# Reordering VectorE and ScalarE work in an attention unit: times-v ahead of the split of q and k, the maximum behind the blocks of q

## What is computed

```python
# layer 0 (layers 1 and 3: no rope, an rmsnorm of q and k instead)
q = (query @ Wq).reshape(nb, q_len, H, D).transpose(0, 2, 1, 3)
k = (key @ Wk).reshape(nb, q_len, KVH, D).transpose(0, 2, 1, 3)
v = (value @ Wv).reshape(nb, q_len, KVH, D).transpose(0, 2, 1, 3)
q = q * cos + _rotate_half(q) * sin
k = k * cos + _rotate_half(k) * sin
scores = jnp.einsum('bhqd,bhkd->bhqk', q, k) / jnp.sqrt(jnp.float32(D))
scores = jnp.where(mask == 0, jnp.float32(-1000000000.0), scores)
attn = jax.nn.softmax(scores, axis=-1)
x = jnp.einsum('bhqk,bhkd->bhqd', attn, v)
return x.transpose(0, 2, 1, 3).reshape(nb, q_len, H * D) @ Wo
```

## Time and profile before

| | us |
|---|---|
| median of 3 runs | 2640.58 |
| lowest, highest | 2638.4, 2644.09 |
| the profiled execution | 2624.64 |
| its span, first to last instruction | 2622.8 |
| PE busy | 2339.1 (89%) |
| DVE busy | 1885.0 (72%) |
| POOL busy | 1551.6 (59%) |
| ACT busy | 1228.2 (47%) |

### The profile page before, as it was taken

The page is one execution under the profiler, slowest core; times in us unless marked ns, Lnnn a source line. Parts: engine busy times, 40 slices in busy tenths (PEclk is TensorE's granted clock), DMA queues, the critical chain, the costliest instruction groups (busy, mean ns, idle before and its releaser), DMA issues.

```text
span 2622.8 us, 40547 instructions
## 1 busy us (share of the span) xinstructions
PE 2339.1 (89%) x12225; PEld 1935.5 (74%) x12225; DVE 1885.0 (72%) x3505; ACT 1228.2 (47%) x3610; POOL 1551.6 (59%) x1624
## 2 busy tenths in 40 slices
PE   5899999989889999999787888799779999999977
PEld 4787777777677888888665777676567888887753
DVE  4677777777877788888775776564377888887762
ACT  2444444444334666666433545323235666665421
POOL 4577777765325677777444666432446777776443
PEclk8899999999999999999899999899989999999989
DMA  3256667665324555555420000149714555554354
GB/s 106 76 188 212 214 212 221 213 198 173 102 73 146 172 178 170 174 173 179 154 68 30 1 1 17 62 153 345 253 57 142 179 178 175 177 173 150 114 200 148
DMA packets 296365, 390.33 MB, mean 149 GB/s; under 512 B 20977, under 2 KB 195697, under 8 KB 293210
## 3 DMA queue, kind: packets, MB, share of 16 engines
q1 hardware_dynamic: 280416, 338.60, 39.7%
q0 software_dynamic: 10224, 42.03, 4.7%
q10 hardware_dynamic: 5514, 7.11, 0.8%
HBM read 269.92 MB, written 151.49 MB: 161 GB/s over the span
## 4 chain that ended last, share of the span: by engine, by line
DMA 16%; POOL 14%; DVE 13%; PE 11%; issue 10%; ACT 4%; SPq 0%; ACTq 0%; DVEq 0%; POOLq 0%
DMA q_in<-between_q 5%; PE B_qkv L841 5%; DMA between_q<-xn 4%; DMA slots_y<-S 3%; POOL qT_l L2252 3%; POOL W L2292 2%; POOL ring_l L2228 2%; DVE ss L1614 2%; DVE qk L1643 2%; DMA out_x<-rows_last 2%; DVE S L1700 1%; DVE S L1697 1%; DVE xn L1666 1%; POOL rn L2239 1%; PE B_out L841 1%
## 5 line engine op out<-in xcount | busy, mean ns | idle before, releaser
L1376 ACT ACTIVATE W<-S,nmx 128x128 f32<-128x128 f32 x768 | 298.5, 395 | 79.3 <-DVE nmx L1703 78.7
L2292 POOL TENSOR_TENSOR W<-W,rden 128x512 f32<-128x512 f32 x192 | 199.8, 1040 | 215.8 <-DVE rden L1708 215.7
L2298 POOL TENSOR_TENSOR pT_l<-W,pT_h 128x512 fp32r<-128x512 f32 x184 | 238.6, 1297 | 48.7 <-ACT pT_h L1197 48.4
L1718 DVE STREAM_TRANSPOSE S<-W 128x512 f32<-128x512 f32 x184 | 130.6, 710 | 189.0 <-POOL W L2292 189.0
L2252 POOL TENSOR_TENSOR qT_l<-q_in,qT_h 128x512 fp32r<-128x512 f32 x156 | 202.6, 1299 | 88.1 <-ACT qT_h L1197 86.7
L2228 POOL TENSOR_TENSOR ring_l<-raw,ring_h 128x512 fp32r<-128x512 f32 x166 | 216.0, 1303 | 61.2 <-ACT ring_h L1197 60.8
L841 PE MATMUL B_out<-ring_h,oT_h 128*128 128x512 f32 x516 | 211.9, 411 | 16.3 <-DVE oT_l L1522 9.5
L898 PE MATMUL B_s<-kT,qT_h 128*128 128x256 f32 x768 | 198.5, 336 | 30.8 <-DVE xnT_l L1522 13.4
L841 PE MATMUL B_out<-ring_h,oT_l 128*128 128x512 f32 x516 | 203.3, 394 | 0.0
L841 PE MATMUL B_out<-ring_l,oT_h 128*128 128x512 f32 x516 | 202.9, 393 | 0.0
L898 PEld LDWEIGHTS B_s<-kT,qT_h 128*128 128x128 f32 x768 | 147.6, 192 | 65.9 <-issue 42.4
(11 more groups left out here) (504 smaller groups left out, 7820.3 us busy)
## 6 DMA issues: line engine op xcount, KB each, us to landing
raw<-in_pieces SPq DMA_DIRECT2D x270, 256.0 KB, 3.0
between_q<-xn SPq DMA_DIRECT2D x156, 320.0 KB, 3.0
q_in<-between_q SPq DMA_DIRECT2D x156, 320.0 KB, 3.3
between_p<-S SPq DMA_DIRECT2D x184, 256.0 KB, 2.7
W<-between_p SPq DMA_DIRECT2D x184, 256.0 KB, 2.8
slots_x<-in_zero SPq DMA_DIRECT2D x32, 1030.0 KB, 7.3
raw<-in_experts SPq DMA_DIRECT2D x16, 768.0 KB, 6.7
w<-in_experts SPq DMA_DIRECT2D x8, 1024.0 KB, 13.9
```

The costliest lines, as they stand in the source:

```text
L1376: t = act.activation(probs_r, scores_r, ACT.Exp, bias=nmx[:, k, r:r + 1], accum_out=den[:, k, r:r + 1])
L2292: pool.tensor_tensor(W3, W3, rden[:, k, :].unsqueeze(2).to_broadcast([P, R, P]), ALU.mult).then_inc(*probs.now((layer, u)))
L2298: pool.tensor_tensor(heads_first(pT[1][:, :]), by_block(W[:, k, :]), heads_first(f32(pT[0][:, :])), ALU.subtract).then_inc(*p_split.now((l ...
```

## The change

Three due numbers change and one step is cut in two.

- `blocks_q` of layer 0 stands at 10.2 instead of 11, and so ahead of `add_out` (10.5).
- The maximum is a step of its own, `max`. For the units turned by DMA it stands at 10.4 in iteration i+3, behind `normalise` (10) and `blocks_q` (10.2) of a later unit; the two mask passes stay at 4. For the other units it directly follows the mask as before.
- `times_v` of units 5 to 56 stands at 12.5 instead of 20: ahead of `split_k`, `split_q`, a weight split and `exp`. PE's order and POOL's stay as they were in steady units; on ACT the copy oT_h moves from behind the exponentials to ahead of the copies of k and q, and on DVE oT_l moves ahead of kT's low part.

```diff
             if (layer, u) in TURNED_BY_DMA:
-                self.at(i + 1, 10.2 if KINDS[layer] == "norm" else 11, "blocks_q", layer, u)
+                self.at(i + 1, 10.2, "blocks_q", layer, u)
...
                 self.at(i + 3, 4, "mask", layer, u)
+                self.at(i + 3, 10.4, "max", layer, u)
                 self.at(i + 3, 16, "exp", layer, u)
...
                 self.at(i + 2, 56, "mask", layer, u)
+                self.at(i + 2, 56, "max", layer, u)
                 self.at(i + 2, 71, "exp", layer, u)
...
-            self.at(i + lag - 1, 20, "times_v", layer, u)
+            self.at(i + lag - 1, 12.5 if u + lag - 3 in range(NB, LAST_BY_DMA + 1) else 20, "times_v", layer, u)
...
                 dve.scalar_tensor_tensor(out=S3, in0=score_parts[:, :, 0, :], scalar=SCALE, in1=S3, op0=ALU.mult, op1=ALU.add
                                          ).then_inc(*sc_read.now((layer, u)))
+
+            def largest(layer, u):
+                k = unit(layer, u)[3]
+                S3 = per_head(S[:, k, :])
                 dve.wait_ge(*sc_read.of((layer, u)))
                 dve.tensor_reduce(nmx[:, k, :], S3, AX, ALU.max, negate=True).then_inc(*maxed.now((layer, u)))
```

More of the change, by code:

```diff
@@ L2190, in vector_program @@
                      "ln_stats": ln_stats, "ln_apply": ln_apply, "ln_turn": ln_turn, "split": split, "project": project,
-                     "normalise": normalise, "fill_tables": fill_tables, "turn_q": turn_q, "blocks_q": blocks_q, "split_k": split_k, "mask": mask,
+                     "normalise": normalise, "fill_tables": fill_tables, "turn_q": turn_q, "blocks_q": blocks_q, "split_k": split_k, "mask": mask, "max": largest,
                      "probs": denominators, "turn_p": turn_p, "blocks_p": blocks_p, "times_v": times_v, "add_out": output, "low": low,
```

## The result

The changed kernel is slower, by 0.4%. Its median is 2650.64 us (2643.72 to 2655.37, 7 runs), against 2638.4 us for the kernel before, measured beside it (2629.92 to 2644.09, 7 runs). The ratio is 1.0041, 95% interval 1.0022 to 1.006. The forecast was 2613, with a range from 2588 to 2646 and a chance of 0.72 on faster, so sign and range are both wrong.

The account below looks back on a forecast made before the run. TensorE, busy 89% of 2622.8 us, was taken as the bound, with only its gaps to win. Terms -24-2-2+0 = -28 us from 2624.64 give 2596.6; plus 15.94 to the median, 2613, range 2588 to 2646.

Parts of the forecast that it names:

- Layer 0, forecast -24: Layer 0's clearing stretch: 21 cheaper pairs of units save 29.4 us, about 5 taken off; ends -16 and -34.
- the pair of units at 18.0 us: Layer 0 with clearings: two successive units cost 18.0 us (10.0 and 8.0) instead of 19.40.
- The p path: Layer 0, probabilities' transposition through DMA store and load to the rotation behind the next transposition: 10.48 us, forecast 10.0.
- rival B: Gain hidden: q's earlier store and load meet the clearing and p's load, p path about 11 us; 2641, chance 0.19.
- the late q: Layer 0: q's late load delays ACT's exponentials; some 26 us of excess, mostly this, taken as gone.
- The low end of the range, -16: Layer 0's smallest gain, -16 us, if the p path stays at 10.5 us.
- Layers 1 and 3, forecast 0: Port hits on kT_l offset gains in other units: 0 us, bounds -18 (no hit) to +20.
- The hits: Layers 1 and 3: kT_l caught behind POOL's weight product in about every second affected unit, 9.4 us against 8.9.
- 8.55 instead of 8.7 to 8.9: Layers 1 and 3: units whose kT_l is not caught were to run at TensorE's 8.55 us.
- The start of the sum: Whole kernel: sum starts from the profiled 2624.64 us; the median's 15.94 above it is carried over.
- C: Slower: kT_l caught in every affected unit of layers 1 and 3, 57 x 0.55 = 31 us; about 2656, chance 0.16.

Follow-up runs that it names:

- after_kT_first: The changed kernel with DVE making kT's low part ahead of oT_l again, ACT's order as changed; ratio to the kernel before 1.0036 (1.0017 to 1.0055).
- after_clear_last: The changed kernel with each clearing issued behind p's load (74 instead of 47), still in layer 0; ratio to the kernel before 1.0208 (1.0177 to 1.0239).

## Why the prediction was wrong

**What bounds the kernel**: right. PE is the bound, and the changes show only in its gaps.

**Layer 0, forecast -24, measured +4.1.** What came as forecast: the store of q earlier, the exponentials soon behind the maximum (from the maximum's end to their start 21.6 us in 39 units before, 9.3 after), DVE's wait for oT_h gone, DVE's wait for v_h grown. The step that failed is the pair of units at 18.0 us. Two things in it were wrong.

- The p path was taken from 10.5 to 10.0, with "nothing" as its worst end. It grew to 11.39 (mean, from 10.67), so the bound had no end on the bad side. Its parts, in units with a clearing: transposition to store of p 0.91 to 1.35 us, store to load of p 3.53 to 3.80, load to pT_h 5.23 to 5.31. The prediction thought that the earlier store of q would shorten this path, and rival B that it would lengthen it; neither is what the runs show. Times-v alone, with q's store in its old place, gives 11.59, and q's blocks alone 10.78.
- The sum made of each relieved wait a relieved unit. Its own undisturbed pair is 10.48+8.12 = 18.60 us, so 0.80 of the 1.40 us that a pair was to gain is the late q, 26 us taken as gone with the wait. The exponentials did come sooner behind the maximum, and nothing was gained; with times-v alone at 13.7 they came later (48.6 us in 39 units) and layer 0 was the shortest of all with the clearings in it, 369.1. That lateness did not set the pace. And the kernel before without a single clearing in layer 0 takes 353.6/39 = 9.07 us per unit, and after 9.02. I had forecast 9.0 with all the clearings still there. In that kernel ACT still waits 178.5 us for q's load, so most of this wait is neither the clearings' doing nor time lost:

```profile
ACT kT L1197 <- DMA q_in<-between_q: 178.5, 45, 5.6
```

Taking the clearings away altogether brings 21.5 us; -24 was more than their whole cost. (The low end of the range, -16, does not follow from its own terms either: 21 x (19.40-18.5) - 5 is 13.9.)

And one price was left at nothing: oT_l ahead of kT_l on DVE was weighed for layers 1 and 3 but not for layer 0. Within the full change it costs 7.3 us there, the largest single term that a run shows; oT_h ahead of the copies on ACT costs 0.6. Blocks of q were moved ahead of the output's addition at no price. Alone they cost 3.5 us, and 9.2 with times-v at 13.7; by which way is not shown. Behind them the maximum now also waits while they wait for POOL's rotation (0.18 above, 12.1 us over the page's group), but with the blocks moved alone that wait is 2.8 us.

**Layers 1 and 3, forecast 0 with bounds of -18 to +20, measured +10.1.** The hits came as described, at 9.48 us (9.4 forecast), with others escaping after a stretched unit, and fewer than thought: 15 of the 48 units with a weight product in the two layers, not every second. What failed is the term on the other side, "8.55 instead of 8.7 to 8.9" for the units that are not hit. Measured over units 15 to 54 of both layers:

| units | before | after |
|---|---|---|
| caught behind the weight product | 34 at 8.81 us | 15 at 9.48 |
| weight product, not caught | 14 at 8.71 | 33 at 8.70 |
| no weight product | 30 at 8.60 | 30 at 8.67 |

The units that were not hit gained nothing. Had these 63 run at 8.55, the two layers would have lost 1.5 us instead of 10.1. The reason was named ("ACT now waits for times-v of this unit before it touches k and q") but priced only through kT_l: qT_l starts later by the same cause, and `after_kT_first` shows that its lateness makes long units without any catch at the weight product. That kT_l would be held less did happen (median 880 to 651 ns) and brought nothing.

The Trainium skill's rule ("SBUF — State Buffer", section "SBUF: two separate sides"), that the second of the two instructions stands still while the first holds the port pair, agrees again with the trace of after: 1.20 us beside the weight product, 0.371 at best. That the hit sets the time is not part of the rule, and `after_kT_first` shows that it need not.

**The start of the sum.** The 15.94 between the profiled execution and the median was carried over; the medians lie 2650.64 - 2638.4 = 12.2 apart, so the sum that would have been right is +14 in the three layers. A second profile of the same kernel would have shown that 6 us of the distance lie between layers 1 and 3.

**Rivals.** The time lies between B (2641) and C (2656), and neither is what happened. B's p path of about 11 us came, but not by B's way, q's store brought forward. C's catch in every affected unit did not come (15 of 48). Both stood on a known hazard; the delay of q and k itself, on ACT in layers 1 and 3 and on DVE in layer 0, was in neither.

**Open.** Times-v's move makes the p path grow; how that divides between SP's order and the queueing in the DMA engines was not tried apart. A longer p path is not by itself a longer layer: with times-v alone at 13.7 it took 10.81 us, and layer 0 was 6 us shorter than before. Whether ACT's or DVE's order makes the loss when times-v is moved alone was not tried. The layer times are of one profiled execution each, and the split of layer 0 rests on them, since the ratios of after and after_kT_first (1.0041 and 1.0036) do not part the two; differences of 1 to 2 us among the kernels at 13.7 are within what was not repeated.

## What to carry to other kernels

Before a step is moved ahead on an in-order engine, list what stands behind its wait, and price the delay for each of those consumers, on each engine that the step touches, not only for the one with a known hazard: here times-v behind the two copies and kT_l instead of ahead of them turned +0.33% into -0.37%. When a wait vanishes, ask what the time would be if its cause were taken away altogether, and let no forecast go under that. And two delays need not add: the maximum's, free beside times-v at 12.5, cost 3.8 to 5.2 us a layer once times-v stood at 13.7.

## What the runs showed of the hardware

A DVE instruction held at the port is long in the profile rather than idle ahead of it: kT's low part is an instruction of 0.371 us that reads 1.20 us, and it ends 0.16 us behind POOL's product (1201.13 against 1200.97), so the list of waits shows nothing of it on DVE, and puts the scores' wait for it down to "issue" ([0.76 <-issue] above). And transfers issued behind a 1030 KB copy take much longer: in after p's load takes 5.27 us to pT_h with the clearing ahead of it and 2.89 without, and q's store to load takes 7.37 us directly behind a clearing and 3.55 in the units between (after_clear_last). The same clearings cost 21.5 us in layer 0 of before but 42.1 in layer 1 (381.8-339.7).
